# Preparing the next batch of an attention stage through another PSUM bank, in other slots, and a wider table lookup

## The reference

```
x = x + attention(layernorm(x))      # 4 batches of 512 tokens, 16 heads
x = x + ffn(layernorm(x))            # 688 hidden, weights looked up in a table of 16
x = x + ssm(layernorm(x))            # a scan along the tokens
x = x + ffn(layernorm(x))

attention: q_c  = rms_norm(x @ wq_down.T) (192)      kv_c = rms_norm(x @ wkv_down.T) (64)
           k_rope = rope(x @ wk_rope.T) (64), one for all heads
           q = [q_c @ wq_up.T | rope(q_c @ wq_rope.T)],  k, v = kv_c @ wkv_up.T
           softmax(q k^T / sqrt(192), causal) v @ wo.T
ffn:       w = lut[idx];  (silu(x w_gate) * (x w_up)) w_down
```

## Time and profile before

| | |
|---|---|
| median of three runs | 858.46 us |
| the profiled execution | 856.87 us |
| its span, first to last instruction | 855.1 us |
| attention's units, first to last query product | 39.0 to 553.5 us |
| lookup on GpSimd | 35.9 to 580.2 us |
| last addition of attention's output | 594.6 us |
| TensorE, VectorE, ScalarE, GpSimd busy | 89, 79, 71, 59% of the span |
| granted TensorE clock | 1.00 in most of the span, 0.66 from 60 to 80 us |

### The profile page before, as it was taken

How to read it: one execution, slowest core, us unless ns; L and a number is a source line. 1 busy time by engine, 2 the same in 40 slices (tenths; PEclk the granted TensorE clock), 3 DMA queues, 4 the chain that set the end, 5 groups by cost and what they waited for, 6 DMA issues and landing times.

```text
span 855.1 us, 15304 instructions
## 1 busy us (share of the span) xinstructions
PE 763.9 (89%) x4556; PEld 652.0 (76%) x4556; DVE 677.1 (79%) x2216; ACT 609.8 (71%) x1500; POOL 503.8 (59%) x543
## 2 busy tenths in 40 slices
PE   4767988899988899988899999997898999999998
PEld 3656767777877687877777788876787887987987
DVE  3676879898879899888989899896666778777643
ACT  3455888888888888888888799995435675665232
POOL 1599999999999999999999999981000000000000
PEclk9786999999999999999999999999999999999999
DMA  9800000000000000000000100000000000000000
GB/s 248 253 1 1 1 1 2 1 2 2 2 1 2 1 1 2 2 1 2 1 1 1 38 2 1 2 1 1 1 1 1 1 1 2 1 1 25 26 26 25
DMA packets 15377, 14.53 MB, mean 17 GB/s; under 512 B 5792, under 2 KB 14432, under 8 KB 15040
## 3 DMA queue, kind: packets, MB, share of 16 engines
q1 hardware_dynamic: 13792, 11.41, 4.6%
q0 software_dynamic: 624, 2.12, 0.7%
q10 hardware_dynamic: 880, 0.04, 0.1%
HBM read 11.46 MB, written 2.10 MB: 16 GB/s over the span
## 4 chain that ended last, share of the span: by engine, by line
PE 56%; DVE 16%; issue 13%; ACT 13%; DMA 0%; DVEq 0%; SPq 0%; ACTq 0%
PE bank L614 12%; PE bank L616 11%; PE bank L615 11%; PE bank L1442 4%; ACT prob L797 4%; ACT prob L817 3%; DVE pt_lo L1127 2%; PE bank L1456 2%; PE bank L1459 2%; ACT pt_hi L826 2%; PE bank L579 2%; DVE o_b L1133 1%; PE bank L1469 1%; DVE bias_m L1075 1%; PE bank L1471 1%
## 5 line engine op out<-in xcount | busy, mean ns | idle before, releaser
L745 POOL TENSOR_SCALAR hot<-raw_gu,lut 128x256 f32<-128x256 int32 x165 | 193.3, 1171 | 16.7
L751 POOL TENSOR_TENSOR total<-total,hot 128x256 f32<-128x256 f32 (+1 forms) x238 | 173.2, 728 | 19.9
L1075 DVE CUSTOM_DVE_ANT_0 bank<-bank,mask 128x128 f32<-128x128 f32 (+3 forms) x256 | 126.2, 494 | 39.6 <-issue 37.3
L797 ACT ACTIVATE prob<-bank,bias_m 128x128 f32<-128x128 f32 (+3 forms) x256 | 136.1, 532 | 23.4 <-DVE bias_m L1075 22.7
L1127 DVE TENSOR_TENSOR pt_lo<-bank,pt_hi 128x512 fp32r<-128x512 f32 x160 | 108.9, 681 | 9.9 <-ACT pt_hi L826 9.7
L1442 PE MATMUL bank<-ident,prob 128*128 128x128 f32 x640 | 98.5, 276 | 15.3 <-ACT prob L817 10.4
L817 ACT ACTIVATE prob<-prob,rden 128x128 f32<-128x128 f32 (+3 forms) x224 | 105.4, 536 | 6.1 <-DVE rden L1110 5.6
L614 PE MATMUL bank<-kt_hi,qt_hi 128*128 128x128 f32 (+3 forms) x256 | 89.5, 350 | 19.8 <-DVE xt_lo L588 5.0
L826 ACT CAST pt_hi<-bank 128x512 fp32r<-128x512 f32 x160 | 93.5, 585 | 15.3 <-PE bank L1459 9.8
L745 POOL TENSOR_SCALAR hot<-raw_dn,lut 128x256 f32<-128x256 int32 (+1 forms) x90 | 97.2, 1080 | 9.1
L1442 PEld LDWEIGHTS bank<-ident,prob 128*128 128x128 f32 x640 | 73.0, 140 | 32.0 <-ACT prob L817 16.9
(11 more groups left out here) (207 smaller groups left out, 2096.0 us busy)
## 6 DMA issues: line engine op xcount, KB each, us to landing
x<-in_L_attn_a_x_dram SPq DMA_DIRECT2D x4, 512.0 KB, 7.9
wo_nat<-in_L_attn_a_wo_dram SPq DMA_DIRECT2D x1, 2048.0 KB, 12.5
out_dram<-x SPq DMA_DIRECT2D x16, 128.0 KB, 1.8
wqu<-in_L_attn_a_wq_up_dram SPq DMA_DIRECT2D x2, 768.0 KB, 8.2
wqr<-in_L_attn_a_wq_rope_dram SPq DMA_DIRECT2D x4, 192.0 KB, 7.4
raw_dn<-in_L_ffn_down_idx_dram POOLq DMA_DIRECT2D x1, 688.0 KB, 10.3
raw_gu<-in_L_ffn_gate_idx_dram POOLq DMA_DIRECT2D x1, 640.0 KB, 7.3
raw_gu<-in_L_ffn_up_idx_dram POOLq DMA_DIRECT2D x1, 640.0 KB, 8.0
```

The costliest lines, as they stand in the source:

```text
L745: nc.gpsimd.tensor_scalar((hot if v else total)[:, 0:n], raw[:, c:c + n], float(v), lut[:, v:v + 1], ALU.is_equal, ALU.mult).then_inc(lut_ ...
L751: nc.gpsimd.tensor_tensor(dst, total[:, 0:n], hot[:, 0:n], ALU.add).then_inc(lut_sum, 1)
L797: nc.scalar.activation(prob[:, n % 2, h, 0:w], bank[2 + h % 2][:, 0:w], ACT.Exp, bias=bias_m[:, n % 2, h:h + 1], scale=-1.0, accum_out=den ...
L1075: nc.vector.tensor_tensor_reduce(out=bank[2 + h % 2][:, 0:w], in0=bank[2 + h % 2][:, 0:w], in1=mask[:, TB * P - w:TB * P], scale=1.0, scal ...
```

## The change

It moves the preparation to bank 1 (that of the query transposes) and to other steps: one down product in each of slots 4 to 7, token steps in slots 8 to 11 (six each), x in slots 9 and 10, features in slots 12, 13 and 14, the value split in 15. In the loop slots 4 to 7 are steps 20 to 23 of the batch before; for batch 1 they are steps 4 to 7 of the lead-in. Key features and values get a second set each. TensorE's wait ahead of these is now for the low part of the query transposes (`qt_lo_s`), and the wait for the copy or the low part stands ahead of the next query transpose. The normalisation of x is spread over slots 4 to 7. The lookup's chunks are 704 columns wide instead of 256 (four and two chunks instead of eleven and six), and its two scratch tiles lie where the state-space weights come later; the tasks that load those wait for all sums. In the lead-in the split of batch 1's x moves a few places within step 3.

```
-TOKEN_AT = (0, 1, 3, 4, 7, 8, 10, 11)
+TOKEN_AT = (0, 2, 3, 7, 8, 10)
+NORM_AT = (1, 4, 5, 9, 11)
+def ahead(s, b, nb):
+    u, m = (s, b + 1) if s < UNITS + 4 else (s - UNITS, BATCH if nb is None else nb + 1)
+    return (u, m) if m < BATCH else (-1, None)
...
+        lut_at = keep.at
         ssm_hi = keep("ssm_hi", [P, 3, CK, DIM], F32R)
...
-        kt_hi = r2("kt_hi", [P, SEQ], F32R)
-        kt_lo = r2("kt_lo", [P, SEQ], F32R)
-        v_hl = r2("v_hl", [P, TB, 2, KR], F32R)
+        kt_hi = r2("kt_hi", [P, 2, SEQ], F32R)
+        kt_lo = r2("kt_lo", [P, 2, SEQ], F32R)
+        v_hl = r2("v_hl", [P, 2, TB, 2, KR], F32R)
...
-        GC = GT * DIM // 11
-        hot = r2("hot", [P, GC], F32)
-        total = r2("total", [P, GC], F32)
+        GC = GT * DIM // 4
+        hot = nc.alloc_sbuf_tensor_at("hot", [P, GC], F32, offset=lut_at)
+        total = nc.alloc_sbuf_tensor_at("total", [P, GC], F32, offset=lut_at + 4 * GC)
...
                     e.wait_ge(wkn_in, 16)
+                if S0 <= k < F0:
+                    e.wait_ge(lut_sum, gu_sums + dn_sums)
...
-            return bank[3 if b else 2 + t % 2]
+            return bank[1 if b else 2 + t % 2]
...
-            o = bank[3 if b and k < 2 else k]
+            o = bank[1 if b else k]
...
# act_slot
-                if nb is not None and s in (8, 9):
-                    down_copy(nb, 2 * (s - 8))
-                if nb is not None and s == 18:
-                    feature_high(nb, 2)
                 do(q_copy, s)
-                if nb is not None and s in (8, 9):
-                    down_copy(nb, 2 * (s - 8) + 1)
-                if nb is not None and s in (10, 11):
-                    act_xt_part(nb + 1, s - 10, bank[3])
-                if nb is not None and s in (13, 14):
-                    feature_high(nb, s - 13)
+                u, m = ahead(s, b, nb)
+                if 4 <= u <= 7:
+                    down_copy(m, u - 4)
+                if u in (9, 10):
+                    act_xt_part(m + 1, u - 9, bank[1])
+                if 12 <= u <= 14:
+                    feature_high(m, u - 12)
                 do(normalise, s - 3, 0)
...
# dve_slot
-                    if nb < BATCH - 1:
-                        if s == 9 and 3 <= k < 3 + TB:
-                            at_norm(nb + 1, k - 3)
-                    elif s in (8, 9):
...
-                        ln_step(GAPS * (s - 8) + k, nb + 1, (nb + 1) % BATCH)
-                    if s in (10, 11, 12) and k in TOKEN_AT:
-                        token_step(len(TOKEN_AT) * (s - 10) + TOKEN_AT.index(k), nb)
+                    if 4 <= u <= 7 and m + 1 < BATCH and k == 5:
+                        at_norm(m + 1, u - 4)
+                    if 4 <= u <= 7 and m + 1 == BATCH and k in NORM_AT:
...
+                        ln_step(len(NORM_AT) * (u - 4) + NORM_AT.index(k), BATCH, 0)
+                    if 8 <= u <= 11 and k in TOKEN_AT:
+                        token_step(len(TOKEN_AT) * (u - 8) + TOKEN_AT.index(k), m)
...
-                if nb is not None and s == 18:
-                    feature_low(nb, 2)
                 do(row_max, s - 2, 0)
-                if nb is not None and s in (10, 11):
-                    dve_xt_part(nb + 1, s - 10, bank[3])
-                if nb is not None and s in (13, 14):
-                    feature_low(nb, s - 13)
+                if u in (9, 10):
+                    dve_xt_part(m + 1, u - 9, bank[1])
+                if 12 <= u <= 14:
+                    feature_low(m, u - 12)
...
                 between(10)
+                if b == 0 and s == 3:
+                    dve_xt(1)
                 do(qt_low, s - 1)
...
-                if nb is not None and s == 19:
-                    split_values(nb)
+                if u == 15:
+                    split_values(m)
...
# pe_slot
-                if nb is not None and s in (9, 10):
-                    pe.wait_ge(dp_cp, nb * TB + 2 * (s - 8))
-                if nb is not None and s in (11, 12):
-                    pe.wait_ge(xt_lo_s, 2 * nb + 2 + s - 10)
-                if nb is not None and s in (14, 15):
-                    pe.wait_ge(at_lo, 3 * nb + s - 13)
                 do(scores, s - 3, 1)
                 do(values, s - 5, 1)
+                u, m = ahead(s, b, nb)
+                if 5 <= u <= 8:
+                    pe.wait_ge(dp_cp, m * TB + u - 4)
+                if u in (10, 11):
+                    pe.wait_ge(xt_lo_s, 2 * (m + 1) + u - 9)
+                if 13 <= u <= 15:
+                    pe.wait_ge(at_lo, 3 * m + u - 12)
                 do(q_transpose, s - 2)
...
                 do(p_transpose, s - 4, 1)
+                if 4 <= u <= 7 or u in (9, 10) or 12 <= u <= 14:
+                    pe.wait_ge(qt_lo_s, 1 + b * UNITS + s - 1)
+                if 4 <= u <= 7:
+                    if u == 4:
+                        wait_xt(pe, m)
+                    down(m, u - 4)
+                if u in (9, 10):
+                    pe_xt_part(m + 1, u - 9, bank[1])
+                if 12 <= u <= 14:
+                    if u == 12:
+                        pe.wait_ge(tok, 1 + 14 * m + 12)
+                    to_features(m, u - 12)
                 do(project, s - 6)
                 do(p_transpose, s - 4, 2)
-                if nb is not None and s in (8, 9, 10, 11, 13, 14):
-                    pe.wait_ge(s_exp, 1 + b * HEADS * TB + G * (s - 2))
...
                 do(scores, s - 2, 0)
-                if nb is not None and s in (8, 9):
-                    pe.wait_ge(dp_cp, nb * TB + 2 * (s - 8) + 1)
-                    down(nb, 2 * (s - 8) + 1)
```

More of the change, by code:

```diff
@@ L576, in pe_xt_part @@
                 nc.tensor.wait_ge(ln_norm, p * TB + TB)
-            nc.tensor.wait_ge(xt_lo_s, 2 * p + (c if o is bank[3] else 0))
+            nc.tensor.wait_ge(xt_lo_s, 2 * p + (c if o is bank[1] else 0))
             for t in range(TB):
@@ L645, in feature_major @@
         def feature_major(b, k):
-            o = bank[3 if b and k < 2 else k]
+            o = bank[1 if b else k]
             return ((qa_hi[:, b % 2, :], o[:, :], qa_lo[:, b % 2, :], qa_hi[:, b % 2, :]),
                     (qb_hl[0:QB, b % 2, :], o[0:QB, :], qb_hl[QB:P, b % 2, :], qb_hl[0:QB, b % 2, :]),
-                    (kt_hi[:, :], o[:, :], kt_lo[:, :], kt_hi[:, :]))[k]
+                    (kt_hi[:, b % 2, :], o[:, :], kt_lo[:, b % 2, :], kt_hi[:, b % 2, :]))[k]
         primed = {
@@ L1059, in split_values @@
                 kv = cd[:, :, QR:QR + KR]
-                nc.vector.tensor_copy(v_hl[:, :, 0, :], kv).then_inc(tok, 1)
+                nc.vector.tensor_copy(v_hl[:, b % 2, :, 0, :], kv).then_inc(tok, 1)
                 dve.wait_ge(tok, 1 + 14 * b + 13)
-                nc.vector.tensor_tensor(v_hl[:, :, 1, :], kv, v_hl[:, :, 0, :], ALU.subtract).then_inc(tok, 1)
+                nc.vector.tensor_tensor(v_hl[:, b % 2, :, 1, :], kv, v_hl[:, b % 2, :, 0, :], ALU.subtract).then_inc(tok, 1)
             def feature_low(b, k):
@@ L1144, in do @@
                     step_of(b, nb, step, n, *k)
+                u, m = ahead(s, b, nb)
                 def between(k):
-                    if nb is None:
-                        return
-                    if nb < BATCH - 1:
-                        if s == 9 and 3 <= k < 3 + TB:
-                            at_norm(nb + 1, k - 3)
-                    elif s in (8, 9):
-                        if s == 8 and k == 0:
+                    if 4 <= u <= 7 and m + 1 < BATCH and k == 5:
+                        at_norm(m + 1, u - 4)
+                    if 4 <= u <= 7 and m + 1 == BATCH and k in NORM_AT:
+                        if u == 4 and k == NORM_AT[0]:
                             dve.wait_ge(x_add, 1 + TB)
-                        ln_step(GAPS * (s - 8) + k, nb + 1, (nb + 1) % BATCH)
-                    if s in (10, 11, 12) and k in TOKEN_AT:
-                        token_step(len(TOKEN_AT) * (s - 10) + TOKEN_AT.index(k), nb)
+                        ln_step(len(NORM_AT) * (u - 4) + NORM_AT.index(k), BATCH, 0)
+                    if 8 <= u <= 11 and k in TOKEN_AT:
+                        token_step(len(TOKEN_AT) * (u - 8) + TOKEN_AT.index(k), m)
                 if s >= 2:
@@ L1221, in _ @@
                         at_norm(1, t)
-                if s == 3:
-                    dve_xt(1)
             for b in range(BATCH - 1):
@@ L1428, in scores @@
                 split_mm(bank[2 + h % 2][:, 0:w],
-                         [(qt_hi[:, n % 2, h, :], qt_lo[:, n % 2, h, :], kt_hi[:, 0:w], kt_lo[:, 0:w])],
+                         [(qt_hi[:, n % 2, h, :], qt_lo[:, n % 2, h, :], kt_hi[:, b % 2, 0:w], kt_lo[:, b % 2, 0:w])],
                          True, True).then_inc(s_mm, 1)
@@ L1453, in values @@
                     pe.wait_ge(tok, 1 + 14 * b + 14)
-                v = v_hl[:, j, :, :].rearrange("p a r -> p (a r)")
+                v = v_hl[:, b % 2, j, :, :].rearrange("p a r -> p (a r)")
                 pe.wait_ge(pt_hi_s, b * BLOCKS + c + 1)
@@ L1496, in pe_slot @@
```

(19 more changed lines are left out.)

## The result

The changed kernel takes 863.45 us (median of 20 runs), the kernel before 857.5 in as many. The ratio is 1.0072, with a 95% interval from 1.0057 to 1.0087: slower by 6 us, where 3.5 us faster was forecast. That is on rival (b)'s side.

The account below looks back on a forecast made before the run. No engine is idle for long (TensorE busy 764 of 855 us), so gains must come from single stages. 856.9 minus 19.0 plus 15.4 is 853.3; the median lies 1.6 higher, so 855 us, own range 850 to 860, whole range 841 to 872.

Parts of the forecast that it names:

- rival (b): Shared SBUF port of VectorE and GpSimd: wider lookup wins, kernel slower; net +3 or +13, middle 866 us, chance 0.29.
- Parts 1 and 2: Attention's preparation, moved to bank 1 and spread over slots: 6.35 us gained per batch, 19 us in all, bounds 7 to 28.
- the wait for the low part: TensorE's wait for the query transpose's low part, slots 4 to 7: priced at zero, bound 6 us per batch.
- the failing cover: Down-product matmuls on TensorE, slots 4 to 7: free while it awaits normalisations; 4.8 us if that cover fails.
- Part 3, the width of compares and adds, the lookup's end: GpSimd's lookup at 704 columns: compares 2.61 us, adds 1.73 us, six chunks ending near 457 us instead of 580.
- Part 3, the hold on the port: Shared SBUF port: adds shut VectorE out for 1.62 us, compares for 0.91; 0.27 us more wait per operation.
- Part 3, the give-back of 15.4 us: VectorE's added port waits in attention: 5.9 us lost per batch, over 2.8 batches 16.6, minus 1.2, gives 15.4 us.
- the share of 0.61: Attention slots: average part of VectorE's blocked time that lengthens a slot, used to price the added waits.
- two twins: Slots 1 and 2 of batch 1, each against its twin: 0.68 us paid for 0.74, and 0.31 for 1.04.
- Its direct worth is zero: Lookup's earlier end gains nothing: feed-forward preparation waits for attention's end near 594 us anyway.
- Rival (a): Attention's new slots: ScalarE binds, so only a third of VectorE's stalls count; give-back 6, net -13, 845 us, chance 0.27.
- Rival (c): Waits only move from bank 3 to bank 1; 1 us per batch won, net +12, 871 us, chance 0.08.

## Why the prediction was wrong

The forecast's net of -3.6 us came out as +6.0, and the miss is smaller than the errors in it: the gain was forecast 9 us too small and the give-back 19 us too small. In its own terms, with VectorE's stretch taken as its busy time less that of the same placement without a lookup, and the cost as the time less that of the same kernel:

| kernel | VectorE stretched, us | lookup costs, us | cost per us of stretch |
|---|---|---|---|
| before, 256 columns | 20.3 | 13.2 | 0.65 |
| before, 704 | 48.9 | 35.3 | 0.72 |
| new placement, 256 | 24.1 | 25.9, 9.2 of it the lookup's end | 0.69 without that |
| new placement, 704 (the change) | 60.2 | 47.8 | 0.79 |
| new placement, 704, compares only | 11.9 | 7.2 | 0.61 |

The costs are medians of 4 to 20 runs, the stretches come from one execution each. A microsecond or two in a cost moves the shares of the 256-column rows and the last one by 0.1 or more, so these shares alone don't tell the placements apart; the slots above do.

- **Parts 1 and 2, the gain of 19 us: right in kind, too small.** It is 28.1 us without a lookup, and 24.7 at 256 columns if the 9.2 us of the lookup's end are added back: at the far end of the bounds (7 to 28). The lower of these bounds left out two that the text names, the wait for the low part (6 us per batch) and the failing cover (4.8); neither was needed. Slots 4 to 7 were forecast near 26.5 and take 25.93; slots 12 to 14 were 25.9 (24.06 plus 1.8) and take 25.42. Slots 8 and 9 were 13.65 and take 12.97, 10 and 11 16.4 and take 14.76. The value split in slot 15 was priced at 0.8 and costs nothing (8.07 against 8.11). Slot 2 was 9.3 and takes 8.31. The small and the large token steps fit into VectorE's gaps better than charged.
- **Part 3, the width of compares and adds, the lookup's end: right.** 457 us was forecast for the end; the last sum ends at 461.0.
- **Part 3, the hold on the port: nearly right, the total of the stretch right in part by luck.** Adds hold it for 1.56 us (forecast 1.62), compares for 0.64 (0.91). Extra stretch was 51 x 0.27 x 2.8 = 38.6 us in the forecast, less some at the end; it grew by 60.2 - 20.3 = 39.9. But the q_tok sums, 12 us of the forecast, took 24.4 of it ((57.0 - 27.2) less (32.6 - 27.2), 27.2 being their time without a lookup), and all the other operations 15.5 instead of 26.5. Random arrivals at the measured holds would wait (1.56^2 + 0.64^2) / (2 x 4.52) = 0.31 us. Ahead of the lookup's end the sums wait 0.29 us in the mean in the old placement at 704 columns, as the model has it, and 0.62 in the new one.
- **Part 3, the give-back of 15.4 us: the step that failed.** "Some 15 lie in slots 4 to 8, where ScalarE's added time covers them; 36 count", and the share of 0.61. Together they let 16.6 of 38.6 us of stretch through, 0.43 of it. Against the kernel before, the lookup costs 34.6 us more for 39.9 us more of stretch: 0.87. Compare the changed kernel's stretches with those of its twin without a lookup. In slots 4 to 7 VectorE is busy 7.8 us longer in three batches, which costs 2.8: over half is covered, as argued. In slots 8 to 14 it is busy 32.5 us longer, and they last 31.1 us longer: a share of 0.96. The 0.61 was the mean of two twins at 0.92 and 0.30 in the old placement, and it fits that placement: there slots 8 to 14 pay 0.59, and slots 8 and 9 nothing. The new placement takes its gain out of the engines' idle time, and in slots 8 to 11 that was what had hidden VectorE's waits. The 34.6 us against 28.1 gained are the 6 us.
- **What the forecast had no term for: TensorE's clock.** In slots 12 to 14 of batch 2 the changed kernel's TensorE is busy 26.42 us for work that takes 24.84 in the twin. It had stood idle for 1.62 us behind the late rotation of the queries, and then ran at 1.2 GHz until about 423 us (granted clock 0.50):

```profile
419.41 0.59 PE L1410 MATMUL bank<-wa_hi,qa_hi 128*128 128x512 f32 x1 [1.62 <-DVE q_rot L1100]
```

  Two more such stretches lie between 250 and 330 us; the twin without a lookup has none between 90 us and its last query product. Each costs TensorE 1.6 to 2.0 us of busy time, and from 30 to 90 us the clock averages 0.77 instead of 0.83. By the same estimate as above (16.0 us against 7.2) at most some 9 of the 47.8 us are the clock's. No run takes them out.
- **"Its direct worth is zero": right against the kernel before, incomplete.** The new placement at 256 columns would have waited 9.2 us for the lookup's end. That is why the measured 21.9 us for the width is less than the port alone would take (about 31).
- **Rival (b)** named the place, and its first form (all 51 operations count, net +3) is 2 us low. Its second form, a compare that shuts VectorE out for 1.8 us, is refuted by the 0.64. Its price of 866 is the middle of the two, so that it lies within 2.5 us is in part luck. **Rival (a)** falls: in slots 8 to 14 hardly a stall was hidden. **Rival (c)** falls, though its sign, slots 12 to 14 above 28 us, was missed narrowly (27.92): the placement gains in every comparison. The rule of the Trainium skill, page SBUF — State Buffer, Who interferes with whom, that the port is kept for the whole instruction, comes close for adds (1.56 of 1.71 us). For compares the trace disagrees (0.64 of 2.64 us), and so does the kernel with compares only, at 822.93 us.

## What to carry to other kernels

A background task that nobody waits for can still set the time, through a lock that it holds: keep the instructions that hold it longest (here adds of two tiles) short enough for the slack of what they block, and only as wide as it takes for the task to end in time. When a change fills idle time, price every other wait again with that idle time gone; here a share of 0.59 in the loose schedule became 0.96 in the same slots of the tight one. And run a bundle's parts alone: here one was worth 15 to 28 us and the other cost 22.

## What the runs showed of the hardware

- A GpSimd add of two tiles shut out VectorE's sum of two SBUF tiles for 0.59 of 0.72 us at 256 columns and 1.56 of 1.71 at 704. A compare with one tile shut out the same sum for 0.33 of 1.14 us at 256 columns, and a pair of VectorE's normalisations for 0.64 of 2.64 at 704. Each figure is one place in a timeline; that no sum beside compares alone took more than 0.96 us agrees. With one input moved to PSUM, the same VectorE sum took 424 ns in the mean of 64, beside the same lookup.
- In the new placement the waits are not those of random arrivals (0.62 us in the mean of 48 sums, against 0.31). In slots 12 and 13 of batch 0 two successive sums each began just after an add, and took 1.88 and 1.75 us; the two adds start 9.12 us apart, two of GpSimd's pairs of compare and add, and those slots are 9.21 and 9.03 us long (timeline of the changed kernel, VectorE's rows, then GpSimd's):

```profile
149.74 1.88 DVE L1102 TENSOR_TENSOR q_tok<-q_tok,q_rot 128x256 f32<-128x256 f32 x1
158.99 1.75 DVE L1102 TENSOR_TENSOR q_tok<-q_tok,q_rot 128x256 f32<-128x256 f32 x1
...
149.62 1.71 POOL L762 TENSOR_TENSOR total<-total,hot 128x704 f32<-128x704 f32 x1
...
158.74 1.72 POOL L762 TENSOR_TENSOR total<-total,hot 128x704 f32<-128x704 f32 x1
```

  That the two schedules lock onto each other is argued from this, not tested.
